# Blanking the padding rows of 32 expert lists: seventeen wide transfers during the run, or thirty-two narrow ones behind the last row of each list

## The reference

```
x = x + attention(layernorm(x))                  # (1, 2048, 256)
h = rmsnorm(layernorm(x)) * norm_w
scores = softmax(h @ router_w.T)                 # 32 experts
topk_w, topk_ids = top_k(scores, 4); topk_w /= sum(topk_w)
sort_idx = argsort(topk_ids); xs = h[sort_idx // 4]      # 8192 rows, grouped by expert
g, u = split(ragged_dot(xs, w1, group_sizes))
ys = ragged_dot(silu(g) * u, w2, group_sizes)
routed = sum over the token's 4 rows of topk_w * ys
out = x + routed + (silu(h @ sg) * (h @ su)) @ sd
```

## Time and profile before

| | us |
|---|---|
| three timed runs, median | 1118.99 |
| the profiled execution: its time | 1115.1 |
| its span, first to last instruction | 1113.4 |
| its mean granted TensorE clock, of full speed | 0.859 |
| busy: PE / DVE / ACT / POOL | 969.2 / 672.8 / 491.2 / 620.2 |

### The profile page before, as it was taken

How to read it: one execution, slowest core, us unless ns; L and a number is a source line. 1 busy time by engine, 2 the same in 40 slices (tenths; PEclk the granted TensorE clock), 3 DMA queues, 4 the chain that set the end, 5 groups by cost and what they waited for, 6 DMA issues and landing times.

```text
span 1113.4 us, 31656 instructions
## 1 busy us (share of the span) xinstructions
PE 969.2 (87%) x12419; PEld 832.0 (75%) x12419; DVE 672.8 (60%) x1626; ACT 491.2 (44%) x938; POOL 620.2 (56%) x775
## 2 busy tenths in 40 slices
PE   3876899998999998899999989997487688999998
PEld 2764688788778788788877877887486355888887
DVE  6368947665766767586576658557824244444446
ACT  4533345453544545454354536343142222555552
POOL 3031238866885886787588568753314111665663
PEclk8687879779887988988797799869678798999999
DMA  6647027339565943946694380011052904444558
GB/s 244 205 101 210 1 50 196 116 101 252 156 177 153 275 135 89 282 119 182 171 255 135 78 229 16 25 50 35 30 209 75 362 29 133 134 148 149 154 183 294
DMA packets 181617, 165.32 MB, mean 148 GB/s; under 512 B 75219, under 2 KB 173916, under 8 KB 180576
## 3 DMA queue, kind: packets, MB, share of 16 engines
q10 hardware_dynamic: 70768, 72.65, 23.1%
q1 hardware_dynamic: 103072, 73.78, 22.4%
q0 software_dynamic: 7632, 16.87, 4.6%
HBM read 65.76 MB, written 101.55 MB: 150 GB/s over the span
## 4 chain that ended last, share of the span: by engine, by line
PE 49%; POOL 18%; DVE 12%; issue 8%; ACT 2%; DMA 2%; SPq 0%; POOLq 0%; DVEq 0%; ACTq 0%
PE ps L1653 7%; POOL arena L810 7%; POOL arena L807 6%; PE ps L1678 4%; PE ps L1563 4%; DVE arena L1146 4%; POOL nrm L773 3%; PE ps L1472 3%; PE ps L1428 3%; PE ps L1482 3%; PE ps L1492 3%; PE ps L1580 3%; PE ps L1644 2%; PE ps L1461 2%; PE ps L1541 2%
## 5 line engine op out<-in xcount | busy, mean ns | idle before, releaser
L1146 DVE SCALAR_TENSOR_TENSOR arena<-ps,cw,arena 128x256 f32<-128x256 f32 x384 | 155.3, 474 | 43.3 <-ACT arena L932 43.3
L1428 PE MATMUL ps<-work,arena 128*128 128x259 f32 x512 | 161.5, 472 | 15.4 <-DVE arena L1146 9.7
L1428 PEld LDWEIGHTS ps<-work,arena 128*128 128x128 f32 x512 | 117.1, 238 | 43.2 <-DVE arena L1146 11.2
L862 POOL DMA_INDIRECT picked<-work x95 | 94.3, 993 | 77.9 <-issue 57.1
L851 POOL DMA_INDIRECT slotted<-hr,slots x64 | 63.5, 993 | 101.7 <-DVE slots L1297 85.6
L810 POOL TENSOR_TENSOR arena<-arena 128x31 f32<-128x31 f32 (+15 forms) x186 | 109.9, 591 | 14.6
L1335 DVE TENSOR_TENSOR work<-work,ps 128x128 f32<-128x128 f32 (+1 forms) x111 | 34.1, 307 | 125.8 <-ACT work L1043 120.1
L807 POOL TENSOR_TENSOR arena<-arena 128x31 f32<-128x31 f32 (+15 forms) x186 | 95.0, 511 | 12.4
L1653 PE MATMUL ps<-arena,work 128*128 x380 | 97.8, 380 | 0.0
L932 ACT ACTIVATE arena<-ps,cw 128x256 f32<-128x256 f32 x128 | 58.0, 472 | 87.7 <-PE ps L1428 72.8
L832 POOL TENSOR_TENSOR work<-work,ec 128x512 f32<-128x512 f32 x32 | 34.0, 1062 | 88.8 <-PE ps L1521 66.2
(11 more groups left out here) (231 smaller groups left out, 2215.4 us busy)
## 6 DMA issues: line engine op xcount, KB each, us to landing
slotted<-blank ACTq DMA_DIRECT2D x17, 4128.0 KB, 18.9
arena<-in_w SPq DMA_DIRECT2D x2, 6528.0 KB, 27.3
arena<-tab SPq DMA_DIRECT2D x96, 128.0 KB, 4.5
work<-slotted SPq DMA_DIRECT2D x95, 129.0 KB, 2.1
arena<-picked SPq DMA_DIRECT2D x8, 1024.0 KB, 14.5
work<-tab SPq DMA_DIRECT2D x32, 128.0 KB, 3.7
arena<-in_w_qkv SPq DMA_DIRECT2D x1, 2048.0 KB, 7.5
xin<-in_x SPq DMA_DIRECT2D x16, 128.0 KB, 5.2
```

Source lines behind the costliest of these rows:

```text
L862: g.indirect_dma_start(out=picked, out_offset=bass.IndirectOffsetOnAxis(ap=to, axis=0), in_=yrow(j), in_offset=None, bounds_check=TOPK * T ...
L1146: v.scalar_tensor_tensor(out=acc_, in0=bank_of("proj", p, s_, i)[:, k:k + W2], scalar=cw[:, u, k:k + 1], in1=acc_, op0=ALU.mult, op1=ALU.a ...
L1428: ins = mm(to[:, 0:WX], wqkv[:, k, m:m + P], xt2[:, p % 3, k, :], start=k == 0, stop=k == KD - 1)
```

## The change

The stages `blank` and `blanks` are gone, with the 17 transfers on ACT's queue, ACT's waits ahead of them, and the wait for them in `send`. Instead `lists` on DVE first adds, for each expert, its count of rows to its start: `gap_first` holds the first row behind the last one of each expert, and `gap_at` the same plus the partition's number. Behind the last `send`, POOL waits for these and scatters the tile `blank` to the 128 rows behind the last row of experts 0 to 11. SP does the same for experts 12 to 31 with plain transfers, whose first row it reads into a register, eight at a time. SP then waits as before for the table, for the now 76 scatters and 21 blanking transfers, and loads the tiles.

```diff
+GAPS_ON_POOL = 12
-    "blank": [(-30.4,)],                       (and in END_0, END_1)
-    "blanks": [(199.2, 0), (235.3, 1)],        (and in END_0, END_1)
 # SP, behind the schedule
+            sp.wait_ge(S["rows_out"], 1)
+            for e in range(GAPS_ON_POOL, E):
+                k = (e - GAPS_ON_POOL) % AHEAD
+                if k == 0:
+                    gaps = nc.values_load_multi_w_load_instructions(
+                        gap_first[0:1, e:min(e + AHEAD, E)], engines=(mybir.EngineType.SP,), min_val=0, max_val=E * STRIDE - P,
...
+                sp.dma_start(slotted[bass.ds(gaps[k], P), :], blank).then_inc(S["blank_sent"], 16)
             sp.wait_ge(S["table_out"], 1)
-            sp.wait_ge(S["sent"], 16 * TOPK * NB)
-            sp.wait_ge(S["blank_sent"], 16 * (NB + 2))
+            sp.wait_ge(S["sent"], 16 * (TOPK * NB + GAPS_ON_POOL))
+            sp.wait_ge(S["blank_sent"], 16 * (1 + E - GAPS_ON_POOL))
 # POOL, stages
-                    pool.wait_ge(S["blank_sent"], 16 * (b + 2))
...
+                if name == "lists":
+                    pool.wait_ge(S["rows_out"], 1)
+                    for e in range(GAPS_ON_POOL):
+                        g.indirect_dma_start(out=slotted, out_offset=bass.IndirectOffsetOnAxis(ap=gap_at[:, e:e + 1], axis=0),
+                                             in_=blank, in_offset=None).then_inc(S["sent"], 16)
 # ACT, stages
-                if (name, *ix) in BLANKS:
-                    t = BLANKS[name, *ix]
-                    act.wait_ge(S["blank_sent"], 16 * (t + 1))
-                    act.dma_start(by_rank[t * P:(t + 1) * P, :, :],
-                                  blank.unsqueeze(1).broadcast_to([P, E, WIDE])).then_inc(S["blank_sent"], 16)
 # DVE, lists
+                v.tensor_tensor(gap_first, total, expert_at, ALU.add)
+                done(v.scalar_tensor_tensor(out=hot[:, 0, :], in0=total, scalar=me, in1=expert_at, op0=ALU.add, op1=ALU.add))
+                v.tensor_copy(gap_at, hot[:, 0, :]).then_inc(S["rows_out"], 1)
 # PE, rows
-                    pe.wait_ge(S["rows_out"], 1)
+                    pe.wait_ge(S["rows_out"], 2)
```

More of the change, by code:

```diff
@@ L59 @@
     "xload": [(-30.4,)],
-    "blank": [(-30.4,)],
     "mul": [(-29.2, 0, 0), (-28.8, 0, 1), (-23.7, 1, 0), (-23.3, 1, 1), (-18.9, 2, 0), (-18.5, 2, 1), (-9.3, 3, 0), (-8, 3, 1),
@@ L126 @@
     "send": [(199.1, 0), (235.3, 1)],
-    "blanks": [(199.2, 0), (235.3, 1)],
 }
@@ L201 @@
     "send": [(188.9, 0), (235, 1)],
-    "blanks": [(189, 0), (235.1, 1)],
 }
@@ L276 @@
     "send": [(177.5, 0), (200.5, 1)],
-    "blanks": [(177.5, 0), (200.5, 1)],
 }
@@ L281 @@
 PER_BLOCK = ("osq", "nin", "npow", "yn", "yt", "yg", "op", "x2", "xin", "lnp", "xn", "rmp", "hh", "base", "hr", "ht", "htb", "rt", "mx", "ex",
-             "tk", "rank", "slot", "send", "blanks")
+             "tk", "rank", "slot", "send")
 FILL = ("nin", "yn", "op", "x2", "xn", "hh", "rt", "mx", "tk", "rank", "slot")
@@ L345 @@
 SCHEDULE = schedule()
-BLANKS = {item: t for t, item in enumerate([item for item in SCHEDULE if item[0] in ("blank", "blanks")][:NB + 1])}
 AFTER_SUM = {"ht": "htb_in", "rt": "rt_in", "rank": "rank_in"}
@@ L555, in gated_delta_moe @@
         lane = sb("lane", 8)
+        gap_at = sb("gap_at", E, dt=U32)
+        gap_first = sb("gap_first", E, dt=I32)
         table = sb("table", 2, P, dt=I32)
@@ L565, in gated_delta_moe @@
         O, U = (KS, QS), (UR, W[3])
-        by_rank = slotted[0:E * STRIDE, :].rearrange("(e r) w -> r e w", e=E)
         s_in, s_wq, s_w, s_pool, s_vch = (sem(n) for n in ("inputs_loaded", "projection_loaded", "weights_loaded", "pool_steps", "vector_steps"))
@@ L691, in _ @@
                 stage(*item)
+            sp.wait_ge(S["rows_out"], 1)
[4 more added lines that the diff above has]
+                        gap_first[0:1, e:min(e + AHEAD, E)], engines=(mybir.EngineType.SP,), min_val=0, max_val=E * STRIDE - P,
+                        skip_runtime_bounds_check_because="an expert has at most T rows of its STRIDE")[1]
+                sp.dma_start(slotted[bass.ds(gaps[k], P), :], blank).then_inc(S["blank_sent"], 16)
             sp.wait_ge(S["table_out"], 1)
-            sp.wait_ge(S["sent"], 16 * TOPK * NB)
-            sp.wait_ge(S["blank_sent"], 16 * (NB + 2))
+            sp.wait_ge(S["sent"], 16 * (TOPK * NB + GAPS_ON_POOL))
+            sp.wait_ge(S["blank_sent"], 16 * (1 + E - GAPS_ON_POOL))
             sent_rows = []
```

## The result

The changed kernel takes 1117.35 us (median of 20 runs, 1113.59 to 1121.3). The kernel before, run beside it, takes 1113.38 (20 runs, 1105.4 to 1121.29). The ratio is 1.0041, with a 95% interval of 1.0022 to 1.0061: slower by 4.0 us between the medians and 4.6 by the ratio, where 12.1 were forecast. The three runs of the kernel before that the forecast started from (1117.88, 1118.99 and 1121.29) are among the twenty, at their upper end.

What follows compares the result with a forecast made beforehand. The prediction took PE (49% of the chain of waits) and POOL (18%) as bounding, DMA only 2%. It added 14.1 at the end, less 2.0 returned ahead: 12.1 on 1118.99 gives 1131 us, range 1121 to 1139 for 8 in 10.

Steps and rivals of the forecast that it cites:

- The end, 14.1: From the last block's counts to tile 0: PE starts 11.8 later, plus 2.3 for the lowered clock, 14.1 us later.
- a bound 1.2 beyond it: At the end: bytes on the DMA engines land by 946.5, 1.2 beyond POOL's 945.3; kept as the term's upper bound.
- The run ahead of it, 2.0: Pairs of blocks ahead of the end: removing the seventeen transfers and ACT's waits returns 2.0 us, taken between 4.0 and -2.4.
- the sign of a wrong forecast: In the pairs: forecast is wrong if the L1482 groups stand closer by more than 1 per pair.
- POOL's waits of the earlier trace: Four pairs with a late transfer: POOL's waits, 4.0 us in all, are what the change can return this way.
- the opposite reading: DVE's transpose to the next pair's L1482: 61.38 without transfers, 60.79 on the mean with them; return nothing or -2.4.
- The first rival: In the pairs: the seventeen transfers slow every pair, 16.1 us would return, giving 1117.0, not slower; chance 0.12.
- SP as the later of the two: At the end: SP's transfers and POOL's scatters hold each other up, last piece lands 3.8 later, giving 1136.9; chance 0.22.
- PE found no other work: Before tile 0: the rival had PE still running shared blocks, giving at most 3 us back, 1128; chance 0.08.
- The level: Forecast difference of 12.1 us put on the earlier median of 1118.99, giving 1131.1, rounded to 1131.

Runs made afterwards that it cites:

- The run with 8, 12 and 12 pieces: Changed kernel with its 32 blanking pieces behind the lists dealt out as 8 scatters of POOL, 12 transfers of ACT, 12 of SP: 1116.77 us, ratio 0.9991.
- the run with only the pairs' transfers cut: Kernel before, its sixteen wide transfers behind the first cut into four and spread, ACT waiting for the quarter before the last: 1101.46 us, ratio 0.9898.
- with and without them ahead of the new blanking: Kernel before with the new blanking at the end added and the seventeen transfers kept (1133.94 us, ratio 1.0143), beside the changed kernel without them (1.0041).
- the overlapping kernel: Kernel before, but an expert's last tile begins 128 rows ahead of its list's end; only the first transfer stays, no blanking at the end: 1102.28 us, ratio 0.986.
- whole transfers put back: Kernel with overlapping last tiles, all seventeen wide transfers put back at their old places with their waits: 1119.11 us, ratio 1.0022 to the kernel before.
- transfers of 2064 KB, in either form: Kernel with overlapping last tiles, sixteen transfers put back writing half the rows (1129.07 us, ratio 1.0125) or half of each row (1137.94 us, 1.0183).

## Why the prediction was wrong

The direction held; the size did not, 4.0 in place of 12.1. The term that failed is the run ahead of the end.

- **The end, 14.1: right in size, partly by another cause.** Measured from the last block's last scatter to the end of the span, 1113.4 - 927.79 = 185.61 before and 1115.9 - 915.83 = 200.07 after: 14.46 more. PE's tile 0 accounts for 22.12 - 8.83 = 13.29 of it (11.8 forecast), which leaves 1.2 for the clock and all else behind it (2.3 forecast for the clock). The scatters kept their pitch of 1.27 to the hundredth. The landing took 4.09, not 2.3; SP's pitch was 0.62, not 0.54. I had POOL's issuing as what sets the end and the DMA engines as a bound 1.2 beyond it. The run with 8, 12 and 12 pieces shows that the bound is what holds: my 18.9 + 2.4 = 21.3 from the first piece to the last landing was measured as 22.0 and 21.8.
- **The run ahead of it, 2.0: this step failed.** The prediction had "Between 4.0 and -2.4 I take 2.0". The profiles show 11.96, and the run with only the pairs' transfers cut shows 13.2; the timed runs give 14.46 less 4.6, some 10, and 11 to 12 for that run. The pairs' groups of L1482 stand 2.1 closer on the mean (10.4 over five pairs), the sign of a wrong forecast that the prediction had named. What it had at nothing is PE stopping for its own code while a wide transfer is under way. Two readings misled me. POOL's waits of the earlier trace rows are those of a wait that I knew of, ACT's; they leave out PE's idle time put to issue, of which 10.3 went. The share of issue in the chain, 8%, couldn't have told me, for it is 8% after as well; its pieces in the middle of a group of products could. And the opposite reading compared stretches from DVE's transpose to the next pair's group. That part of a pair takes 61.0 after as well: it holds little of the loss (1.44 of 10.4 over five pairs). The rest is in the part ahead of the transpose, 37.37 against 34.43 in one pair.
- **The first rival had it.** "The seventeen transfers slow every pair" came at 10.4 (the groups) to 12.0 (the last scatter) of its 16.1, about the 10.8 at which I let it decide; it named no mechanism. What I held against it was the pair from 622.81 to 721.56, slow with a single transfer. That pair's transfer, of 644.03, is the one that PE's fetch near 658.5 met; it spoke for the rival.
- **The other rivals.** SP as the later of the two: it came true in half. The transfers held each other up, but the last to land was a scatter of POOL's, not a piece of SP's, and only 1.8 behind where I had put POOL's last (19.28 behind the last scatter, 17.5 forecast), not 3.8. PE found no other work: it waited 14.46 against 13.1 forecast.
- **The level.** 1131 was the forecast difference put on a median of 1118.99, where twenty runs give 1113.38. Of the 13.7 between 1131 and 1117.35, 5.6 are this, and 8.1 the step above.

What is shown: the transfers in the pairs cost about 10 to 18 us (10 from the main result less the end; by the ratios, 11 with and without them ahead of the new blanking, 11 for whole ones against quarters in the kernel before, 18 in the overlapping kernel). Bytes, pieces, issues or reads of on-chip memory don't account for it, since the same bytes and pieces in quarters cost nothing that the runs can tell once ACT seldom waits for them. The quarters are both shorter and spread over other places; which of the two helps was not separated. That the link is PE's code is shown by the places where PE stops, always the same ones of its program and a whole number of packets apart, and by the packet due there, which comes later than without transfers. That this is all of the loss is argued: with whole transfers put back PE's idle time accounts for it (10.8 of 11.2 in five pairs), but between the profiles of the two kernels compared here only 2.6 of 10.4 is idle time and the rest the same products taking longer; ACT's wait of 4.9 may have had a part too. Why a packet comes late behind a transfer isn't in the trace, which doesn't show when it was asked for. Open too is why transfers of 2064 KB, in either form, hold PE up longer than whole ones.

## What to carry to other kernels

A large background transfer is not free because the chain of waits shows no DMA: look among PE's waits for idle time put to issue in the middle of a group, and whether a packet of the instruction queue comes just ahead of its end. Cut such a transfer into short pieces (here 1032 KB, 6.2 us to landing), spread them, and let the issuing engine wait only for a piece long landed; here that alone was worth 1%, and pieces of half the size were worse than whole transfers. Before moving work from a covered place to the end, add up its bytes: 4.1 MB behind the last dependency cost 14 us, with the issuing dealt out in either of two ways.

## What the runs showed of the hardware

- Transfers of half the size cost more than whole ones (1.0125 and 1.0183 against 1.0022), and 2064 KB from 64 partitions took 14.6 to land against 19.5 for 4128 KB from 128.
- Read from DRAM in place of on-chip memory, the same write took 26.8 to land against 19.5.
- Kernels with whole transfers spread more from run to run: 1105.4 to 1121.29 before and 1110.17 to 1126.71 in the overlapping kernel, against 1099.4 to 1106.17 there without transfers and 1099.75 to 1104.5 before with quarters. The mean granted clock of the profiled executions doesn't order them: 0.859 before, 0.876 with the whole transfers put back, 0.865 before with quarters.
- Small loads pay for a whole transfer beside them: `xin`, 128 KB, landed in 5.2 before, 6.1 with the transfers put back, 2.0 to 2.1 without, and 2.1 to 2.3 beside quarters and transfers of half the size.
